# Expert network of a transformer block: tokens sorted by expert, weights picked by register, rows moved by indirect DMA

## The chip, the cores and the metric

The kernel runs on one core of one Trainium2 chip. The metric is the device time of one execution in microseconds. Engines: PE (TensorE), DVE (VectorE), ACT (ScalarE), POOL (GpSimd) and SP (SyncE); SP and POOL also issue DMAs. SBUF is the on-chip memory, PSUM holds PE's results.

## What is computed

A block of a transformer in fp32 over x of 8 x 512 tokens with 128 channels: layer norm, causal attention of 16 heads of 8 with relative key and value tables, projection, residual; then layer norm and an expert network of 8 experts, of which each token uses 2, beside 2 shared experts that every token uses.

```python
x = x + attn(layernorm(x))
xt = layernorm(x).reshape(-1, 128)                      # 4096 tokens
scores = softmax(xt @ gate_w.T)
_, idx = top_k(scores + gate_bias, 2)
weights = take_along_axis(scores, idx, axis=1)
for e in range(8):
    gate_e = sum(where(idx == e, weights, 0.0), axis=1)
    y = y + gate_e[:, None] * ((silu(xt @ w1[e].T) * (xt @ w3[e].T)) @ w2[e].T)
z = silu(xt @ sw1.T) * (xt @ sw3.T) @ sw2.T             # 2 x 128 hidden channels
x = x + y + z
```

## The kernel before

Attention works on pairs of batches (GB = 2, so G = 4 groups) and on rows of 128 queries (NI = 4), which makes 16 pairs e of a group and a row. A pair has 8 quads q of four heads; a quad is cut into units m by the width of its row (one unit in row 0, two in row 1, four in rows 2 and 3), 352 units in all. Every engine's program is one loop over slots m, written out at build time. In slot m PE turns the probabilities of unit m-3 (`tp`, L849), does what the plan `OPS[m]` holds and multiplies the scores of unit m+1 (`qk`, L837). `OPS` comes from `schedule()` (L108), which gives each operation a due slot, a rank and one of three spare PSUM banks; where a bank is taken the operation moves to a later slot. Its kinds are relative scores (`rel`), probabilities times values (`av`, L866), values of the near band (`rv`, L882), the turn of y (`yt`, `yb`) and the projection (`pj`, L905). DVE finds the minimum of the scores (L1075) and copies turned probabilities (L1060), ACT takes the exponentials (L998), copies the rest (L987) and the relative scores (L974). POOL has one job a quad, `near_probs` (L783), whose copy of the band (L795, L799) frees one of two buffers of turned probabilities: both copying engines wait for `pc_done` two quads later. SP issues every DMA in order.

Behind attention, `expert_part` (L1142) runs densely: eight chunks of 512 tokens, and in each chunk ten steps, one for each of the 2 shared and 8 routed hidden blocks. A step is two matmuls of 512 columns (`hidden`, L1357 and L1358), Silu on ACT (L1392), the product with the gate half on DVE (L1412), and the second layer as four tiles of 128 tokens (`product`, L1367; the shared blocks accumulate in one product of eight). DVE adds each expert's product, scaled by the token's gate, onto the chunk (L1427); a gate is zero where the token did not pick the expert. h1, h3 and y each have two PSUM banks. The next chunk is normalised on ACT (L1267), turned (L1275), scored (L1290), and its top two experts are found on DVE in some twenty small instructions (L1317 to L1347), all beside the steps of the chunk before. The last attention pair is finished inside the first seven steps (`last_row`). fp32 matmuls stand in the trace as two instructions each, fp32 transposes as one.

## Time and profile before

| | |
|---|---|
| runs | 776.20, 782.39, 783.75 us |
| median | 782.39 us |
| span of the profiled execution | 770.0 us |
| median less span | 12.4 us |
| PE, DVE, ACT, POOL busy in the span | 90%, 77%, 67%, 33% |

A line of the profile names a source line, an engine, what was written and read, the shape and the count, then busy time and the mean of one. Idle time before a group is put to the instruction that ended it. PE's ends are modelled, since matmuls are pipelined: the distance from start to start is what a matmul costs, and the chain of waits shows it.

### The profile page before, as it was taken

The page shows a single profiled execution, that of the slowest core. Times are in us where ns is not written, and L with a number is a line of the kernel's source. Part 1 is how long each engine was busy: PE and PEld are TensorE (multiplying, and loading weights), DVE is VectorE, ACT ScalarE, POOL GpSimd, SP SyncE. Part 2 cuts the span into 40 slices and gives each one's busy share as a digit, 9 for nine tenths or more (in the row PEclk, how much of TensorE's full clock was granted, in tenths as well). Part 3 has the DMA queues.
Part 4 walks back from the last instruction along what each step waited for, and adds up shares of the span by engine and source line. Part 5 has one row for each costly group of instructions (what it writes and reads, how often), then busy time and mean ns, then how long its engine had stood idle before and what let it go on. Part 6 is the DMA issues. An engine that isn't in the chain of part 4 may idle for free. (4 is left out here: it accounts for less than half of the span.)

```text
span 770.0 us, 27094 instructions
## 1 busy us (share of the span) xinstructions
PE 690.5 (90%) x10316; PEld 507.9 (66%) x10368; DVE 589.2 (77%) x2036; ACT 514.7 (67%) x1032; POOL 255.8 (33%) x253
## 2 busy tenths in 40 slices
...
POOL 9443445334355534545543445533000000000000
...
GB/s 255 262 295 335 333 303 264 203 244 277 309 250 302 255 222 253 249 238 241 236 222 266 221 232 255 271 153 50 3 22 28 29 5 23 28 15 1 14 15 14
DMA packets 117839, 138.48 MB, mean 180 GB/s; under 512 B 8976, under 2 KB 86288, under 8 KB 117520
## 3 DMA queue, kind: packets, MB, share of 16 engines
...
## 5 line engine op out<-in xcount | busy, mean ns | idle before, releaser
L1075 DVE CUSTOM_DVE_ANT_0 ps<-ps,near 128x128 f32<-128x128 f32 (+3 forms) x512 | 245.1, 509 | 90.5 <-PE ps L837 57.0
L998 ACT ACTIVATE work<-ps,nmin 128x128 f32<-128x128 f32 (+3 forms) x512 | 248.4, 548 | 54.2 <-DVE nmin L1075 49.4
L849 PE MATMUL ps<-ident,work 128*128 128x128 f32 x1280 | 202.6, 278 | 20.7 <-issue 11.6
L849 PEld LDWEIGHTS ps<-ident,work 128*128 128x128 f32 x1280 | 157.0, 143 | 36.5 <-issue 13.7
L795 POOL TENSOR_SCALAR_AFFINE_SELECT work<-work 128x512 f32<-128x512 f32 x96 | 61.5, 641 | 237.8 <-ACT work L987 203.6
L1392 ACT ACTIVATE near<-ps 128x512 f32<-128x512 f32 x80 | 47.5, 595 | 133.3 <-PE ps L1357 133.2
L799 POOL TENSOR_TENSOR work<-work 128x512 f32<-128x512 f32 x96 | 124.2, 1294 | 8.0
L1060 DVE COPY work<-ps 128x512 f32<-128x512 f32 (+1 forms) x192 | 123.2, 642 | 2.5 <-issue 1.6
L837 PE MATMUL ps<-kb,qb 128*128 128x384 bf16 (+3 forms) x460 | 110.6, 298 | 12.3 <-ACT work L998 9.4
L1367 PEld LDWEIGHTS ps<-work,near 128*128 128x128 f32 x640 | 82.6, 192 | 34.2 <-issue 31.6
L987 ACT ACTIVATE work<-ps 128x512 f32<-128x512 f32 (+1 forms) x160 | 90.2, 564 | 18.7 <-PE ps L849 18.1
L866 PE MATMUL ps<-work,vb 128*9 128x128 f32 x2560 | 96.1, 277 | 4.2 <-ACT relS L974 2.6
L1412 DVE TENSOR_TENSOR near<-near,ps 128x512 f32<-128x512 f32 x80 | 54.9, 687 | 50.3 <-ACT near L1392 36.4
L974 ACT ACTIVATE relS<-ps 128x512 f32<-128x512 f32 x128 | 84.4, 660 | 11.6 <-PE ps L824 10.2
L1367 PE MATMUL ps<-work,near 128*128 128x128 f32 x640 | 83.2, 275 | 0.0
L1357 PE MATMUL ps<-near,work 128*128 128x512 f32 x160 | 82.8, 599 | 0.0
L1358 PE MATMUL ps<-near,work 128*128 128x512 f32 x160 | 81.8, 593 | 0.0
L1427 DVE SCALAR_TENSOR_TENSOR near<-ps,near 128x128 f32<-128x128 f32 x256 | 71.9, 343 | 5.3
L866 PEld LDWEIGHTS ps<-work,vb 128*9 128x9 f32 x2560 | 57.7, 91 | 26.5 <-issue 19.7
L1075 DVE DVE_READ_ACCUMULATOR2_ANT nmin<- 128x1 f32 x512 | 72.1, 141 | 0.0
L882 PE MATMUL ps<-tv,work 128*32 128x8 f32 x4096 | 59.3, 179 | 12.1 <-issue 11.9
L882 PEld LDWEIGHTS ps<-tv,work 128*32 128x32 f32 x4096 | 48.2, 112 | 30.5 <-issue 27.3
...
## 6 DMA issues: line engine op xcount, KB each, us to landing
...
w_slots<-relS SPq DMA_DIRECT2D x128, 256.0 KB, 4.5
qk_rows<-work SPq DMA_DIRECT2D x36, 256.0 KB, 4.7
near<-w_slots SPq DMA_DIRECT2D x32, 256.0 KB, 4.6
qk_rows<-y SPq DMA_DIRECT2D x9, 256.0 KB, 6.8
...
```

Source lines behind the costliest of these rows:

```text
L799: nc.gpsimd.tensor_tensor(dst, ptmp[:, :, :], pT[:, q % 2, :, i * P:(i + 1) * P], ALU.add).then_inc(pc_done, 1)
L837: ins = nc.tensor.matmul(qk_ps[:, m % 3, h * wide:(h + 1) * wide], qb[:, n, i * P:(i + 1) * P], kb[:, n // 4 * 2 + n % 2, 0:wide], start=T ...
L849: ins = nc.tensor.transpose(tp_ps[:, m % 2, n * P:(n + 1) * P], prob[:, m % PROBS, n * P:(n + 1) * P], ident[:, :])
L866: ins = nc.tensor.matmul(bank[32 * h:32 * h + VD, a * P:(a + 1) * P], vb[:, g % 2, b * NI + j, n * VD:(n + 1) * VD], pT[:, q % 2, h, j * P ...
L882: ins = nc.tensor.matmul(bank[32 * tq:32 * tq + NH, a * D:(a + 1) * D], pcT[:, e % 2, tau, :], tv[:, tau, :], start=True, stop=True)
L974: nc.scalar.activation(relS[:, q % RSLOTS, :, :, :].rearrange("p a j h -> p a h j"), misc("rel", q).rearrange("p (a h j) -> p a h j", a=2, ...
L987: nc.scalar.activation(pT[:, q % 2, n * w:n * (w + 1), 0:wide], tp_ps[:, m % 2, 0:n * wide].rearrange("p (h s) -> p h s", h=n), ACT.Copy). ...
L998: ins = nc.scalar.activation(prob[:, m % PROBS, h * wide:(h + 1) * wide], qk_ps[:, m % 3, h * wide:(h + 1) * wide], ACT.Exp, bias=nmin[:, ...
L1060: nc.vector.tensor_copy(pT[:, q % 2, n * w:n * (w + 1), 0:wide], tp_ps[:, m % 2, 0:n * wide].rearrange("p (h s) -> p h s", h=n)).then_inc( ...
L1075: nc.vector.tensor_tensor_reduce(out=scores, in0=scores, in1=near[:, q % NEAR, a, 4 * P - wide:4 * P, r], scale=1.0, scalar=3e38, op0=ALU. ...
L1357: nc.tensor.matmul(h1_ps[k % 2], w1_sb[:, m, :], rhs, start=True, stop=True).then_inc(h1_ready, 1)
L1367: ins = nc.tensor.matmul(y_ps[k % 2][:, n * P:(n + 1) * P], hT[:, (NM * c + m) % 4, n * P:(n + 1) * P], w2_sb[:, m, :], start=(m == ms[0]) ...
```

## The change

The eight routed experts no longer run over all tokens.

- The tokens are taken in three segments: groups 0 and 1 (16 tiles of 128), group 2 (8) and group 3 (8). Within a segment every token's two rows are placed by expert; an expert's rows start at a multiple of 128, so that each tile of 128 rows has one expert. The number of tiles is that of the worst padding: 39, 23 and 23, in units of four tiles 10, 6 and 6, 22 units in all.
- Normalising moves into attention and to POOL (`normalise`: a root by `pow` and a Newton step in small links, then two instructions of 128x128 a pair), for each pair e. SP stores the normalised rows (`xn_dram`), PE turns them (`xt`) and scores them (`gl`) as new entries of the plan, ACT copies the turned rows (stored to `xnT_dram`) and DVE the scores.
- `route` on DVE, once a segment in 19 steps, finds the two experts, the gates, and each row's place: a running sum over tiles, two matmuls for the sum over the 128 partitions (`rk`), and the experts' starts. For segments 0 and 1 it is spread over slots 217 to 238 and 305 to 326 of attention; for segment 2 it is in the tail. Thirty entries of the old plan move by one to three slots.
- POOL scatters the rows: each indirect DMA takes one tile of 128 rows of 512 bytes, for one of the two picks. 32 and 16 of them stand behind the quads 88 to 101 and 120 to 125, up to three a quad, and the last 16 behind attention.
- The tail first runs the 22 sorted units: load, turn (4 transposes), weights of each tile copied by ACT from an offset read into a register (`pick_weights`, four reads and four copies of 128x384), 8 hidden matmuls of 128 columns, Silu, multiply, 4 products, copy, store. Then 16 shared units (dense, 512 columns). POOL gathers the products back, 64 indirect DMAs, chunk by chunk, and DVE adds them with their gates (`combine`) and the shared product (`add_shared`). h1, h3 and the routed y have one PSUM bank each.
- The last attention pair runs in half-steps inside the first sorted units. Square roots on ACT, `normalise` and the exponentials on ACT in the tail but one go away. All expert weights come in one DMA late in attention.

```diff
+SEGMENTS = [(0, 2), (2, 3), (3, 4)]
+SEG = len(SEGMENTS)
+SEG_TILES = [GB * NI * (hi - lo) for lo, hi in SEGMENTS]
+SEG_AT = [GB * NI * lo for lo, hi in SEGMENTS]
+SORTED = [-(-((TOPK * n * P + E * (P - 1)) // P) // 4) for n in SEG_TILES]
+SORTED_AT = [sum(SORTED[:s]) for s in range(SEG + 1)]
+NSORT = SORTED_AT[SEG]
+MOST = max(SEG_TILES)
+SEG_ROWS = GB * 2 * len(Q_PART) * D * H * T * 2 // (4 * C)
...
+    for e in range(LATE):
+        due.append((NORM_AT[e] + 6, 4, ("xt", e)))
+        due.append((NORM_AT[e] + 8, 4, ("gl", e)))
+    for s in range(SEG - 1):
+        due.append((route_slot(s) + 12, 4, ("rk", s)))
...
+SPREAD = [3, 3, 3, 3, 2, 2, 0, 0]
+
+
+def scatters():
+
+    at, q = [[] for q in range(NQ)], 0
+    for s in range(SEG - 1):
+        while q % QUADS or row(q) < 2 or last(q) + 4 < SLOT_OF["rk", s] + 5:
+            q += 1
+        for n in range(TOPK * SEG_TILES[s]):
+            while len(at[q]) >= SPREAD[q % QUADS] or row(q) < 2:
+                q += 1
+            at[q].append((s, n))
+        q += 1
+    return at
+
+
+SCATTER = scatters()
...
+                    for s, n in SCATTER[q]:
+                        experts["scatter"](pool, s, n)
+                experts["normalise"](pool, GI - 1, x1[:, (GI - 1) % 2, :, :], x1_done)
+                for n in range(TOPK * SEG_TILES[SEG - 1]):
+                    experts["scatter"](pool, SEG - 1, n)
+                experts["pool"](pool)
 
...
+                def last_row(half):
 
                     e = GI - 1
-                    if step < 2:
-                        if step == 0:
-                            for kind, *what in LAST:
-                                pe.wait_ge(*READ[kind](*what))
-                            experts["scores"](pe, 0)
-                        for c in range(RVN // 2 * step, RVN // 2 * (step + 1)):
+                    if half < 2:
+                        for c in range(RVN // 2 * half, RVN // 2 * (half + 1)):
                             rv(e, c)
-                    if step in (2, 3):
-                        if step == 2:
-                            experts["wait_turned"](pe, 0)
-                            pe.wait_ge(rvn_done, GI)
-                        else:
-                            experts["wait_scores"](pe, 0)
-                        yt(e, step - 2)
-                    if step == 4:
+                        (xt, gl)[half](LATE)
+                    if half == 2:
+                        yt(e, 0)
+                        yt(e, 1)
+                    if half == 4:
                         yb(e)
-                    if step == 5:
+                    if half == 6:
                         pj(e)
-                    if step == 6:
-                        pe.wait_ge(ynT_done, GI)
-                        pe.wait_ge(x1_done, GI)
+                    if half == 9:
+                        xt(e)
+                    if half == 10:
+                        gl(e)
+                    if half == 16:
+                        rk(SEG - 1)
 
...
+                def last_row(half):
+
+                    s = SEG - 1
+                    if half == 1:
                         near_values(GI - 1)
-                    if step in (2, 3):
-                        normalise(GI - 1, step - 2)
-                    if step == 6:
+                    if half == 3:
+                        experts["copy_scores"](dve, LATE, misc("gl", LATE))
+                        normalise(GI - 1, 0)
+                        normalise(GI - 1, 1)
+                    if half == 7:
                         residual(GI - 1)
-
-                experts["vector"](dve, last_row)
-
-
-def expert_part(nc, ctx, t, ps, x1_dram, gate_w, gate_bias, w1, w3, w2, out):
-    NM = NSH + E
-    CT = CH // P
-    CHUNKS = TILES // CT
-    NY = E + 1
-    AC = 1 + CT * E
+                    if half == 11:
+                        experts["copy_scores"](dve, GI - 1, misc("gl", GI - 1))
+                    if 12 <= half < 16:
+                        for step in ((0,), (1, 2, 3), (4, 5, 6), (7, 8, 9))[half - 12]:
+                            experts["route"](dve, s, step)
+                    if half == 16:
+                        experts["route"](dve, s, 10)
+                    if half in (17, 18):
+                        for step in ((11, 12, 13, 14), (15, 16, 17, 18))[half - 17]:
+                            experts["route"](dve, s, step, misc("rk", s))
+
...
+    def normalise(pool, e, x1, x1_done):
+        if e == 0:
+            pool.wait_ge(const_in, 16)
+            nc.gpsimd.memset(pa[:, 0:pad, :], 0.0)
+            nc.gpsimd.memset(pb[:, 0:pad, :], 0.0)
+        links = [6 * e]
+
+        def then(ins):
+            links[0] += 1
+            ins.then_inc(root, 1)
+            pool.wait_ge(root, links[0])
+
+        pair = tile_pair(e)
+        pool.wait_ge(mv_done, GB * (e + 1))
+        then(nc.gpsimd.tensor_scalar(stat[:, 0, :], mv[:, pair, 1], EPS, None, ALU.add))
+        then(nc.gpsimd.tensor_tensor(stat[:, 1, :], stat[:, 0, :], mhalf, ALU.pow))
+        then(nc.gpsimd.tensor_tensor(stat[:, 2, :], stat[:, 1, :], stat[:, 1, :], ALU.mult))
+        then(nc.gpsimd.tensor_tensor(stat[:, 2, :], stat[:, 2, :], stat[:, 0, :], ALU.mult))
+        then(nc.gpsimd.tensor_scalar(stat[:, 2, :], stat[:, 2, :], -0.5, 1.5, ALU.mult, ALU.add))
+        nc.gpsimd.tensor_scalar(stat[:, 3, :], mv[:, pair, 0], -1.0, None, ALU.mult)
+        then(nc.gpsimd.tensor_tensor(stat[:, 1, :], stat[:, 1, :], stat[:, 2, :], ALU.mult))
+        if x1 is None:
+            pool.wait_ge(xp_in, 16 * EARLY)
+            x1 = xnp[:, e % XN, :, :]
+        else:
+            pool.wait_ge(x1_done, e + 1)
+        if e >= XN:
+            pool.wait_ge(xn_out[e % XN], 16 * (e // XN))
+            pool.wait_ge(xt_ready, e - XN + 1)
+        for b in range(GB):
+            ins = nc.gpsimd.tensor_scalar(xnp[:, e % XN, b, :], x1[:, b, :], stat[:, 3, b:b + 1], stat[:, 1, b:b + 1],
+                                          ALU.add, ALU.mult)
...
+    def scatter(pool, s, n):
+        k, r = SEG_AT[s] + n // TOPK, n % TOPK
+        c = k // NI
+        if n == 0:
+            pool.wait_ge(pos_done, s + 1)
+        if n % (TOPK * NI) == 0:
+            pool.wait_ge(ring_in[c % 2], 16 * (c // 2 + 1))
+        nc.gpsimd.indirect_dma_start(out=sorted_rows, out_offset=bass.IndirectOffsetOnAxis(ap=pos[:, r, k:k + 1], axis=0),
+                                     in_=ring[:, c % 2, k % NI, :], in_offset=None).then_inc(sc_out[c % 2], 16)
 
     def pool_program(pool):
-        for e in range(E):
-            ins = nc.gpsimd.memset(order[:, e:e + 1], float(E - e))
-        ins.then_inc(order_done, 1)
+        for j in range(SORTED_AT[SEG - 1], SORTED_AT[SEG - 1] + XS):
+            load_sorted(pool, j)
+        for s in range(SEG):
+            for n in range(2):
+                pool.wait_ge(y_out[n], 16 * len(range(n, SORTED_AT[s + 1], 2)))
+            for k in range(SEG_AT[s], SEG_AT[s] + SEG_TILES[s]):
+                for r in range(TOPK):
+                    nc.gpsimd.indirect_dma_start(out=yg[:, TOPK * k + r, :], out_offset=None, in_=y_rows[s],
+                                                 in_offset=bass.IndirectOffsetOnAxis(ap=loc[:, r, k:k + 1], axis=0)
+                                                 ).then_inc(yg_in[k // NI], 16)
 
...
+    def tensor_program(pe, last_row):
+        def turn(j):
+            wait_sorted(pe, j)
+            wait(pe, xTs_done, j)
+            for n in range(4):
+                ins = nc.tensor.transpose(tT_ps[:, n * P:(n + 1) * P], xs[:, j % XS, n, :], t["ident"][:, :])
+            ins.then_inc(tT_ready, 1)
+
+        def hidden(j):
+            pe.wait_ge(xTs_done, j + 1)
+            pe.wait_ge(wq_done, j + 1)
+            for w, bank in ((0, h1_ps), (1, h3_ps)):
+                wait(pe, (silu_done, hT_done)[w], j)
+                for n in range(4):
+                    ins = nc.tensor.matmul(bank[:, n * P:(n + 1) * P], wq[j % WQ][:, n, w, :],
+                                           xT[:, j % 2, n * P:(n + 1) * P], start=True, stop=True)
+                ins.then_inc((h1_ready, h3_ready)[w], 1)
+
+        def product(j):
+            pe.wait_ge(hT_done, j + 1)
+            wait(pe, ys_done, j)
+            for n in range(4):
+                ins = nc.tensor.matmul(y_ps[:, n * P:(n + 1) * P], hT[:, j % 2, n * P:(n + 1) * P], wq[j % WQ][:, n, 2, :],
+                                       start=True, stop=True)
+            ins.then_inc(y_ready, 1)
+
+        def hidden_all(u):
+            c, m = divmod(u, NSH)
+            if m == 0:
+                pe.wait_ge(xa_in[c // GB], 32 * GB)
+            for w, bank in ((0, h1_ps), (1, h3_ps)):
+                pe.wait_ge((silu_done, hT_done)[w], NSORT + u)
+                nc.tensor.matmul(bank, ws[:, w, m, :], xnT_all[:, c, :], start=True, stop=True
+                                 ).then_inc((h1_ready, h3_ready)[w], 1)
+
+        def product_all(c):
+            pe.wait_ge(hT_done, NSORT + NSH * (c + 1))
+            if c < 2:
+                pe.wait_ge(ys_done, NSORT)
+            else:
+                pe.wait_ge(acc_done, AC * (c - 1))
+            for n in range(4):
+                for m in range(NSH):
+                    ins = nc.tensor.matmul(ps[:, 4 + c % 2, n * P:(n + 1) * P], hT[:, (NSH * c + m) % 4, n * P:(n + 1) * P],
+                                           ws[:, 2, m, :], start=(m == 0), stop=(m == NSH - 1))
+            ins.then_inc(z_ready, 1)
+
+        turn(0)
+        for j in range(NSORT):
+            if j + 1 < NSORT:
+                turn(j + 1)
+            last_row(2 * j)
+            hidden(j)
+            last_row(2 * j + 1)
+            if j:
+                product(j - 1)
+        for u in range(UNITS2):
+            hidden_all(u)
+            if u == 0:
+                product(NSORT - 1)
+            elif u % NSH == 0:
+                product_all(u // NSH - 1)
+        product_all(B - 1)
+
...
+    def pick_weights(act, j):
+        s = SEG_OF[j]
...
+            act.wait_ge(w_in, 16)
+            offsets.extend(act.alloc_register(f"offset{n}") for n in range(4))
+        if j == SORTED_AT[s]:
+            act.wait_ge(ids_done, s + 1)
+        act.load(offsets, ids[0:1, 4 * j:4 * j + 4])
+        wait(act, y_ready, j - WQ + 1)
+        for n in range(4):
+            at = act.snap(offsets[n], min_val=0, max_val=3 * P * (E - 1))
+            ins = nc.scalar.activation(wq[j % WQ][:, n, :, :].rearrange("p w c -> p (w c)"), wx[:, bass.ds(at, 3 * P)], ACT.Copy)
+        ins.then_inc(wq_done, 1)
 
     def scalar_program(act, last_row):
-        exponentials(act, 0)
-        for k in range(NM * CHUNKS):
-            act.wait_ge(h1_ready, k + 1)
-            wait(act, hT_done, k - 1)
-            nc.scalar.activation(silu[:, k % 2, :], h1_ps[k % 2], ACT.Silu).then_inc(silu_done, 1)
-            last_row(k)
-            if k == NM * (CHUNKS - 4):
-                roots(act, 1)
-            for j in due(k, "normalise"):
-                normalise(act, j)
-            for j in due(k, "copy"):
-                copy_turned(act, j)
-            for j in due(k, "exp"):
-                exponentials(act, j)
-
-    def vector_program(dve, last_row):
-        def hidden(c, m):
-            k = NM * c + m
-            dve.wait_ge(silu_done, k + 1)
-            dve.wait_ge(h3_ready, k + 1)
-            if k >= 4:
-
-                cb, mb = divmod(k - 4, NM)
-                dve.wait_ge(y_ready, NY * cb + max(mb - 1, 0) + 1)
-            nc.vector.tensor_tensor(hT[:, k % 4, :], silu[:, k % 2, :], h3_ps[k % 2], ALU.mult).then_inc(hT_done, 1)
-
-        def add(c, u):
-            k = NY * c + u
-            dve.wait_ge(y_ready, k + 1)
+        def gate(j):
+            act.wait_ge(h1_ready, j + 1)
+            wait(act, hT_done, j - 1)
+            nc.scalar.activation(sl[:, j % 2, :], h1_ps, ACT.Silu).then_inc(silu_done, 1)
+
+        for j in range(NSORT):
+            if j + 1 < NSORT:
+                pick_weights(act, j + 1)
+            gate(j)
+            last_row(j)
...
+        def combine(c, half):
+            if half == 0:
+                dve.wait_ge(yg_in[c], 16 * TOPK * NI)
+                dve.wait_ge(xa_in[c // GB], 32 * GB)
+            for r in range(TOPK):
+                for n in range(2):
+                    k = NI * c + 2 * half + n
+                    if r:
+                        dve.wait_ge(acc_done, AC * c + 4 * half + n + 1)
+                    nc.vector.scalar_tensor_tensor(out=x1_all[:, k, :], in0=yg[:, TOPK * k + r, :], scalar=gates[:, r, k:k + 1],
+                                                   in1=x1_all[:, k, :], op0=ALU.mult, op1=ALU.add).then_inc(acc_done, 1)
+
```

## Rows read from the trace of the kernel before

**Rows 1.** The page, part 2: POOL's busy tenths in 40 slices of 19.25 us.
```profile
POOL 9443445334355534545543445533000000000000
```
**Rows 2.** Windows by stage: stretch, length, busy us (instructions) of each engine, PEclk, DMA share, GB/s.
```profile
20.00:40.00 20.00, 13.87 (x60) 8.63 (x60) 18.82 (x67) 13.11 (x20) 8.53 (x4) 0.87 0.90 266
...
400.00:500.00 100.00, 92.50 (x1935) 72.79 (x1936) 85.78 (x315) 87.14 (x194) 49.15 (x51) 1.00 0.84 249
...
634.00:662.00 28.00, 28.00 (x135) 18.07 (x133) 19.80 (x65) 13.19 (x21) 0.00 (x0) 1.00 0.07 20
```
**Rows 3.** Chain of waits, 634.9 to 665 us: start, us, the piece of the chain.
```profile
635.13 1.78 PE ps L1367 x16
636.91 0.44 PE ps L1275 x4
637.35 0.86 PE ps L1357 x2
...
639.07 0.89 PE ps L1367 x8
...
642.57 0.79 PE ps L1290 x8
...
662.56 1.84 PE ps L1367 x16
```
**Rows 4.** Timeline, PE, the first dense expert matmul: start, us, instruction, shape, count.
```profile
540.10 1.13 PE L1357 MATMUL ps<-near,work 128*128 128x512 f32 x2
```
**Rows 5.** Timeline, the end of the span.
```profile
764.16 0.69 DVE L1412 TENSOR_TENSOR near<-near,ps 128x512 f32<-128x512 f32 x1 [0.65 <-ACT near L1392]
764.99 2.23 DVE L1427 SCALAR_TENSOR_TENSOR near<-ps,near 128x128 f32<-128x128 f32 x8
767.25 0.37 SPq L1233 DMA_DIRECT2D out<-near  x1
```
**Rows 6.** Waits, 130 to 500 us: total us, times, longest.
```profile
DVE ps L1075 <- PE ps L837: 43.4, 62, 2.2
ACT work L998 <- DVE nmin L1075: 34.6, 52, 1.6
```
**Rows 7.** ACT: timeline at 605 us, then groups by shape (busy us, mean ns).
```profile
605.65 1.64 ACT L1267 ACTIVATE near<-vb,work,rstd 128x128 f32<-128x128 f32 x4
...
L987 ACT ACTIVATE work<-ps 128x512 f32<-128x512 f32 x87 | 52.1, 598 | 12.1 <-PE ps L849 11.4
L1015 ACT ACTIVATE work<-ps 128x256 f32<-128x256 f32 x15 | 5.8, 390 | 1.8 <-PE ps L898 1.8
...
L1392 ACT ACTIVATE near<-ps 128x512 f32<-128x512 f32 x80 | 47.5, 595 | 133.3 <-PE ps L1357 133.2
L1392 ACT ACT_TABLE_LOAD x9 | 11.5, 1283 | 0.2
```
**Rows 8.** Timeline, ACT's last copy of attention.
```profile
540.23 0.60 ACT L1010 ACTIVATE y<-ps 128x512 f32<-128x512 f32 x1 [0.42 <-PE ps L866]
```
**Rows 9.** DMA issues: KB each, median us from issue to landing.
```profile
out<-near SPq DMA_DIRECT2D x8, 256.0 KB, 2.3
...
vb<-x_dram SPq DMA_DIRECT2D x6, 256.0 KB, 3.1
```
**Rows 10.** DVE, small instructions: a group by shape, then one line's min/median/max ns.
```profile
L1325 DVE TENSOR_TENSOR near<-near 128x32 f32<-128x32 f32 x8 | 1.5, 192 | 0.3
...
L1100 DVE TENSOR_TENSOR work<-work,rden x32: 291/293/1404, 125.1 to 556.1; 128x128 f32<-128x128 f32 x32
```
**Rows 11.** POOL: timeline of its quads, a group, one line's min/median/max.
```profile
384.99 0.64 POOL L795 TENSOR_SCALAR_AFFINE_SELECT work<-work 128x512 f32<-128x512 f32 x1 [2.97 <-ACT work L987]
...
417.47 0.63 POOL L795 TENSOR_SCALAR_AFFINE_SELECT work<-work 128x512 f32<-128x512 f32 x1 [3.86 <-DVE work L1060]
...
L355 POOL TENSOR_TENSOR work<-work 128x1024 bf16<-128x1024 f32 x6 | 12.8, 2159 | 11.5 <-ACT work L448 11.5
...
L799 POOL TENSOR_TENSOR work<-work x96: 1277/1293/1388, 58.2 to 539.7; 128x512 f32<-128x512 f32 x96
```

728 lines of the change are left out of this document (445 added, 283 removed).

## Prediction

> **What bounds the kernel now.** I read the page's slices first, then the windows by stage, then the chain of waits, and last the waits of the middle. In the slices GpSimd (POOL) is busy until about slice 27 of 40 and then stands at zero: the kernel has two stages, attention up to about 540 us and the expert network behind it [rows 1]. The windows say how the two differ. At 400 to 500 us PE, DVE and ACT are all busy 86 to 93% and the DMA engines 84%; at 634 to 662 us PE is busy all of the time, ACT under half, POOL not at all, the DMA engines 7% [rows 2]. The chain of waits then shows what a dense expert step costs. One chunk of 512 tokens goes from one x16 product (635.13) to the next (662.56): 27.43 us, with ten hidden steps (0.86 for w1, the same for w3), one shared product of 1.78, eight expert products of 0.89, one turn of 0.44 and one score of 0.79: 17.2 + 1.78 + 7.12 + 0.44 + 0.79 = 27.3. Nothing but PE is on it [rows 3]. Eight chunks are 219 us. The first such matmul starts at 540.10 [rows 4]; the last additions start at 764.99, the last store is issued at 767.25, and the trace ends at 770.0 [rows 5]. So the tail is 229.9 us and PE-bound, and fewer products are worth their whole PE time there.
>
> In attention no engine has room of its own: DVE waits for PE 43 us, ACT for DVE 35 us in the 370 us from 130 to 500 [rows 6]. It is a balanced loop, in which work added to any of the three shows in part.
>
> **The sum.** I write the new time as 540.1 (attention now) + a loss in attention + the new tail, and add 12.4 us, by which the median of the runs (782.39) lies above the span (770.0).
>
> **What goes.** 80 hidden steps, 64 expert products and the gate work leave the tail. Sorting needs 22 units of four tiles of one expert each (10 + 6 + 6; the count is fixed by the worst padding), and 16 shared units (two per chunk) stay dense.
>
> **PE of the new tail.** A sorted unit has 4 transposes, 8 hidden matmuls of 128 columns and 4 products. The x8 product entry is four fp32 tiles in 0.89, so the unit is 0.44 + 3 x 0.89 = 3.11 us. Small tiles cost little here: four of 128 columns take 0.89 where one of 512 takes 0.86 [rows 3]. The shared part of a chunk is 4 x 0.86 + 1.78 = 5.22.
>
> **ACT of the new tail.** Each sorted unit copies the weights of four tiles, 128x384 each, in SBUF. Four SBUF-to-SBUF instructions of 128 columns take 1.64 and so stand about 0.4 apart; from 256 to 512 columns a PSUM copy grows by 0.21, so 384 columns add 0.21 and a copy takes 0.60 of the queue. Four are 2.4, Silu 0.5 to 0.6 [rows 7]: 3.0 us, beside PE's 3.11. Unpriced is the reading of four registers from SBUF ahead of them, which no row shows. Its bounds are 0 (ACT's queue still holds copies to run) and, by the nearest fetch that stops ACT, the table load of 1.28 [rows 7]. The banks for h1 and h3 are also single now, so PE waits for Silu. I take 3.7 us a unit, between 3.1 and 4.4. That is 22 x 3.7 = 81.
>
> **Compute path.** The first unit waits for its weight copies behind ACT's last copy at 540.23 (0.6, then 2.4, then about 1 for registers): 4 us [rows 8]. Add 81; 3 for last-row work on PE (rv, yt, pj, the last turns and scores) that the looser loop does not hide; the shared part at 8 x 5.6 = 45 (5.22 and a wait for Silu per chunk); and 4 behind the last matmul (0.69 for the add, 0.37 for the issue, 2.3 for the store's landing [rows 5, 9]). 4 + 81 + 3 + 45 + 4 = 137 us against 229.9. DVE fits: three instructions of 0.69 in a sorted unit, and in a shared chunk eight additions (eight take 2.23 now), two multiplies and one add, 4.3 of 5.6 [rows 5].
>
> **Indirect DMAs on POOL, the price that decides.** The tail holds 16 scatters and 64 gathers, all on one in-order queue, none in the trace of before. Call the queue time of one c. The last segment's positions come with half-step 18 of the sorted loop, that is 9.5 units in: 4 + 9.5 x 3.7 + 3 = 42 us. Then 16c; 4 us for landing and the four sorted loads (a 256 KB load lands in 3.1 [rows 9]); 64c; 2.5 for the last landing (store 2.3 [rows 9]); 7.5 for the last chunk's eight additions, the shared add and the store. Queue path: 56 + 80c. The nearest rows for c are 0.37 (SP issuing a store), 0.63 and 1.29 (one POOL instruction over 128x512) and 2.16 (the longest repeated POOL instruction, 128x1024) [rows 5, 11]. An indirect DMA must be worked out row by row for 128 rows by POOL itself, so the POOL rows are nearer than SP's; I take 1.2 between 1.29 and the shorter ones, and keep 0.4 and 2.16 for the range. At 1.2 the queue path is 152 us, longer than the compute path by 15; they cross at c = 1.01. So the tail is set by POOL's gathers: combine(c) waits for eight gathers a chunk, 9.6 us, where PE needs 5.6. The Trainium skill ("DMA: Bandwidth & Descriptors", Specifications) gives about 1 us to the first byte of a DMA issued from GpSimd; with c = 1.0 the queue path would be 136 and the compute path would end last. No run here shows it yet.
>
> PE then idles over a third of the shared stage. The trace has windows in which PE was busy 69% and the granted clock was 0.87, against 1.00 where it was busy all the time [rows 2]; where the clock falls to 1.2 GHz a chunk's 5.22 becomes up to 10.4, hardly over 9.6. I count it as up to 6 us in the range, not in the sum.
>
> **Attention.** PE gets 14 row pairs of two transposes (0.22) and two score matmuls (a quarter of 0.79 and a load: up to 0.44): 9 us. DVE gets 14 copies and twice about 39 small routing instructions: 0.19 for 128x32 and 0.29 for two SBUF inputs of 128x128 [rows 10], with some 0.03 between them and wider ones for both picks at once, so 13 us for the segment of 16 tiles, 10 for that of 8, 26 with the copies. ACT gets 14 copies of 0.39 [rows 7] and loses two square roots: 3 us. If all of it fits into waits the loss is 0, if PE's and DVE's add up it is 35. DVE has 14 us idle in 100 [rows 2], but the routing comes in bursts of 19 slots that its slack doesn't cover. The DMA engines go from 84% busy to about 90% with some 9 MB more (scatters, stored and reloaded rows). I take 15.
>
> POOL in attention: a quad's own work is 2.0 us (0.63 + 1.29) and quads of the long rows come 5.4 us apart (six in 384.99 to 417.47) [rows 11]. Scatters go up to three behind a quad, 16 a row of eight quads (43 us): 16 + 16c + 6 for two normalisations of about 3. At c = 1.2 that is 41, just inside; it breaks at c = 1.3, and behind a late POOL wait both the copies of the probabilities (pc_done) and PE's turn of the normalised rows. So POOL's work there costs nothing at 1.2, and three rows' overrun, 3 x (16c - 21), above 1.3.
>
> **Sum:** 540.1 + 15 + 152 + 12.4 = 719.5. I predict 720 us, 8% faster.
>
> **Rivals.**
> 1. POOL's DMAs are cheap (c at most 1.0): the compute path ends last. 540.1 + 15 + 137 + 12.4 = 705, and 683 with nothing lost in attention and 3.3 us a unit. For it: a queue that only writes descriptors need not touch 128x512 elements. Against: the POOL rows.
> 2. The register reads stop ACT: 5 us a unit, 110 for the 22, compute path 166, queue path 54 + 96 + 14 = 164. 733. For it: four reads and four addresses a unit stand on ACT's queue in front of copies that PE needs. Against: they can be done while copies run.
> 3. Attention pays 40 rather than 15, since PE waits in line for POOL's rows: 745.
> 4. The slower side: the POOL queue is dear. Its place is the 48 scatters in attention and the 80 DMAs of the tail; the time is 567.5 + 56 + 80c + 48c - 63, equal to 782 at c = 1.73. If each issue also had to wait for one DVE instruction of 0.69, c = 1.2 + 0.69 = 1.9 and the time 804. For it: DVE and POOL do disturb each other, a 128x128 product of two SBUF operands (as in the routing and in combine) takes 0.29 in the median and up to 1.40 [rows 10]. Against: POOL's own 128x512 work keeps to 1.28 to 1.39 there, beside a busy DVE [rows 11]. The Trainium skill ("SBUF — State Buffer", Who interferes with whom) speaks for it: DVE instructions that take both ports keep GpSimd from writing descriptors until they end. Most of DVE's operands here come from PSUM, to which that rule doesn't apply.
> That the change doesn't do what it says has no case: the counts of units are fixed numbers.
>
> **Chances.** Forecast (c from 1.05 to 1.5, 708 to 752) 0.45; rival 1 0.22; rival 2 0.09; rival 3 0.10; rival 4 0.14. The range leaves out rival 4's slower part and the best of rival 1: 685 to 780. Runs of one kernel spread by 1%, so about 1% is what can be told from no change. Rivals 1 to 3 and the forecast are faster by more than that; rival 4 gives 0.12 slower and 0.02 within: 0.85, 0.03, 0.12. Forecast's own range: 708 to 752.
>
> **What would show it.** Each indirect DMA 1.2 us apart on POOL, POOL the releaser of combine in the last 60 us and PE idle there; sorted units 3.7 us apart with ACT busy over 80%; attention ending near 555. Wrong would be: additions that never wait for gathers (rival 1), units 5 us apart (2), pc_done or xn_done among the long waits (3), scatters 1.7 us or more apart (4).

## The result: slower by 7.6%

The kernel after takes 838.85 us (median of 4 runs, 835.08 to 841.95) against 781.4 us for the kernel before beside it (776.2 to 783.75). The ratio on record, of the fast runs of both kernels, is 1.076, with a 95% interval from 1.068 to 1.084 (the two medians alone divide to 1.074). The prediction was 720 us and "faster". The profiled execution has a span of 833.3 us; before it was 770.0 us.

First the page of the kernel after: the span, the slices (20.8 us each) and the groups of the two new operations. The answer to [rows 1] is the POOL line: GpSimd now works until 800 us.

```profile
span 833.3 us, 27048 instructions
PE   4686789999789999887789867878878647144967
DVE  7875668886778787888868467977745623021546
ACT  3686767887778788875557467756665514031211
POOL 8453444344668444654568666445831065745430
PEclk9998999999989999999899999989999888566989
L1507 POOL DMA_INDIRECT sorted_rows<-work x64 | 62.7, 980 | 44.5 <-DVE work L1642 28.1
L1518 POOL DMA_INDIRECT near<-y_rows,work x64 | 60.8, 950 | 43.2 <-DMA y_rows<-work 24.3
```

Two things stand out. The indirect DMAs are as cheap on GpSimd as forecast: 0.95 to 0.98 us each and 0.30 between two. And in slices 35 to 37 (about 708 to 771 us) PE, DVE and ACT all fall to 0 to 4 tenths while GpSimd is at 4 to 7: next to nobody else works. The granted clock falls with them, to 0.5 and 0.6.

The timeline of PE gives the borders of the stages (answering [rows 4]): the first turn of a sorted unit, and the first and last products of the dense shared stage.

```profile
610.70 0.63 PE L1659 MATMUL ps<-ident,kb 128*128 128x128 f32 x4 [0.92 <-ACT y L1129]
773.42 1.88 PE L1686 MATMUL ps<-qb 128*128 128x512 f32 x4
825.12 1.88 PE L1686 MATMUL ps<-qb 128*128 128x512 f32 x4
```

So attention ends at 610.7 us, not at 540.1, and the tail takes 222.6 us, of 229.9 before: 163 for the 22 sorted units and 60 for the shared part. The forecast had 555 and 152.

The windows of these two stages and of the 32 gathers of the first segment (stretch, length, busy us of PE, PE weight load, DVE, ACT, POOL, then PEclk, DMA share, GB/s; compare the dense stage in [rows 2]), then the waits of the last of these stretches:

```profile
696.00:736.00 40.00, 11.40 (x82) 10.22 (x81) 4.43 (x7) 5.51 (x12) 30.32 (x32) 0.65 0.45 123
610.00:773.00 163.00, 93.46 (x891) 88.30 (x892) 53.50 (x116) 55.88 (x118) 69.49 (x80) 0.76 0.43 121
773.00:833.00 60.00, 47.50 (x206) 27.04 (x204) 34.95 (x91) 9.55 (x16) 15.37 (x16) 0.94 0.23 62
```

```profile
DVE work L1762 <- remote: 25.3, 1, 25.3
ACT y L1738 <- remote: 11.5, 1, 11.5
POOL near L1518 <- issue: 9.8, 32, 0.3
```

In those 40 us PE is busy 11.4, DVE 4.4 and ACT 5.5. "remote" stands for a release that the trace cannot find: one multiplication of DVE waited 25.3 us although every instruction it needs had been recorded as ended long before (PE's matmuls at 703.8 us, ACT's Silu at 718.6; the multiplication starts at 735.6). That is the loss, and the experiments are about what it is.

### The profile page after: what moved, and what is told of

Its sections match the earlier page's. It is cut to its first block and busy times, and to the rows that moved or that the text cites. A ratio compares the mean times of both kernels' runs of the same rounds, so it can differ in the third digit from the quotient of the medians.

```text
span 833.3 us, 27048 instructions
## 1 busy us (share of the span) xinstructions
PE 644.8 (77%) x10228; PEld 494.5 (59%) x10228; DVE 545.8 (65%) x1821; ACT 495.7 (59%) x1031; POOL 426.5 (51%) x523
## 5 line engine op out<-in xcount | busy, mean ns | idle before, releaser
L963 PE MATMUL ps<-ident,work 128*128 128x128 f32 x1280 | 210.4, 285 | 29.7 <-ACT work L1106 18.6
L963 PEld LDWEIGHTS ps<-ident,work 128*128 128x128 f32 x1280 | 160.7, 146 | 57.6 <-ACT work L1106 25.3
L951 PE MATMUL ps<-kb,qb 128*128 128x128 bf16 (+3 forms) x512 | 132.6, 311 | 16.7 <-ACT work L1117 13.9
L1185 DVE COPY work<-ps 128x512 f32<-128x512 f32 (+1 forms) x192 | 123.4, 642 | 27.0 <-POOL work L907 19.2
L1093 ACT ACTIVATE relS<-ps 128x512 f32<-128x512 f32 x128 | 84.5, 661 | 15.5 <-PE ps L938 11.9
L1507 POOL DMA_INDIRECT sorted_rows<-work x64 | 62.7, 980 | 44.5 <-DVE work L1642 28.1
L1518 POOL DMA_INDIRECT near<-y_rows,work x64 | 60.8, 950 | 43.2 <-DMA y_rows<-work 24.3
L980 PEld LDWEIGHTS ps<-work,vb 128*9 128x9 f32 x2560 | 58.9, 92 | 30.2 <-issue 22.2
L996 PE MATMUL ps<-tv,work 128*32 128x8 f32 x4096 | 63.8, 181 | 16.3 <-issue 15.0
L1762 DVE TENSOR_TENSOR work<-y,ps 128x512 f32<-128x512 f32 x38 | 26.1, 687 | 75.9 <-remote 31.8
L1738 ACT ACTIVATE y<-ps 128x512 f32<-128x512 f32 x38 | 22.5, 593 | 84.1 <-remote 40.8
L951 PEld LDWEIGHTS ps<-kb,qb 128*128 128x128 bf16 x512 | 42.5, 101 | 37.1 <-ACT work L1117 20.2
L938 PE MATMUL ps<-te,qb 128*128 128x128 bf16 x512 | 51.9, 226 | 10.6 <-ACT relS L1093 7.0
L938 PEld LDWEIGHTS ps<-te,qb 128*128 128x128 bf16 x512 | 35.5, 100 | 26.5 <-issue 14.8
```

Source lines behind the costliest of these rows:

```text
L938: ins = nc.tensor.matmul(bank[:, h * P:(h + 1) * P], qb[:, 4 * u + h, i * P:(i + 1) * P], te[:, :], start=True, stop=True)
L951: ins = nc.tensor.matmul(qk_ps[:, m % 3, h * wide:(h + 1) * wide], qb[:, n, i * P:(i + 1) * P], kb[:, n // 4 * 2 + n % 2, 0:wide], start=T ...
L963: ins = nc.tensor.transpose(tp_ps[:, m % 2, n * P:(n + 1) * P], prob[:, m % PROBS, n * P:(n + 1) * P], ident[:, :])
L980: ins = nc.tensor.matmul(bank[32 * h:32 * h + VD, a * P:(a + 1) * P], vb[:, g % 2, b * NI + j, n * VD:(n + 1) * VD], pT[:, q % 2, h, j * P ...
L996: ins = nc.tensor.matmul(bank[32 * tq:32 * tq + NH, a * D:(a + 1) * D], pcT[:, e % 2, tau, :], tv[:, tau, :], start=True, stop=True)
L1093: nc.scalar.activation(relS[:, q % RSLOTS, :, :, :].rearrange("p a j h -> p a h j"), misc("rel", q).rearrange("p (a h j) -> p a h j", a=2, ...
```

## Experiments

Each time below is that of one run, beside one run of the kernel before on the same chip (777.2 us for the first four, 777.1 or 776.7 for the others). The kernel after was timed beside 781.4, so differences of a few microseconds from its 838.9 say nothing.

### Are the gathers to blame, or do they only make room? Gathers last

GpSimd waits for all sorted products before the first gather.

```
-        for s in range(SEG):
-            for n in range(2):
-                pool.wait_ge(y_out[n], 16 * len(range(n, SORTED_AT[s + 1], 2)))
+        for n in range(2):
+            pool.wait_ge(y_out[n], 16 * len(range(n, NSORT, 2)))
+        for s in range(SEG):
```

> The changed kernel with one difference: POOL starts its 64 gathers only when all 22 sorted products are stored, not segment by segment. Theory A (while DMAs whose descriptors POOL writes are in flight, DVE and ACT start instructions late although all they wait for is done): the units after the 16 scatters take about 3.5 us instead of the 9 us they took beside gathers, the sorted units end near 710 us instead of 780, and the 80 us of gathers then stand behind them: about 815 us in all. Theory B (the sorted units are slow by themselves: single PSUM banks, register reads, stores of products): the sorted units still end near 780, the gathers come on top, and the time is near 875.

854.8 us, against 777.2 for before on the same chip. The windows, with the border of the two stages at 719 us:

```profile
610.00:719.00 109.00, 85.46 (x893) 82.85 (x894) 53.58 (x116) 55.52 (x118) 24.04 (x32) 0.87 0.52 152
719.00:852.00 133.00, 54.73 (x203) 31.40 (x202) 34.92 (x91) 9.55 (x16) 60.78 (x64) 0.69 0.19 52
```

The sorted stage fell from 163 to 109 us once the gathers had left it, and the shared stage, which got all 64 of them, rose from 60 to 133. The loss goes where the gathers go. The total lies between the two expectations (815 and 875), so it did not decide by itself; the stages did: the sorted units end at 719, near theory A's 710 and far from theory B's 780.

### The same gathers in the kernel before

Here nothing of the change is made. 64 indirect gathers of 64 KB are added to GpSimd, which has nothing to do there, from the third dense chunk on. They go from the input into a buffer of attention that is free by then, and nobody reads them. The cut leaves out the load of the indices.

```
+    def extra(pool):
+        pool.wait_ge(spots_in, 16)
+        pool.wait_ge(acc_done, AC * 2)
+        for k in range(64):
+            nc.gpsimd.indirect_dma_start(out=spare[:, k, :], out_offset=None, in_=x_rows,
+                                         in_offset=bass.IndirectOffsetOnAxis(ap=spots_sb[:, k:k + 1], axis=0)
+                                         ).then_inc(extra_done, 16)
```

> The kernel before, with 64 indirect gathers of 128 rows of 512 bytes (from the input x into an SBUF buffer that nothing reads) added on POOL, which is idle there, from the third dense chunk on. The dense steps themselves are unchanged. Theory A: PE, DVE and ACT wait with nothing to wait for while the gathers run (80 us), and the time grows by 30 us or more, to 810 or above. Theory B: the dense steps keep their 27.4 us a chunk and the time stays within 3 us of before, 782.

Two controls move the same bytes at the same place with plain descriptors. In the first GpSimd issues them; in the second SP does.

```
-            nc.gpsimd.indirect_dma_start(...)
+            pool.dma_start(spare[:, k, :], x_rows[P * (k % 32):P * (k % 32 + 1), :]).then_inc(extra_done, 16)
```

> As the run with 64 added gathers, but each DMA is a plain one from POOL (64 KB of consecutive rows of x, no index). Theory A in the form that any DMA with descriptors written by POOL does it: the same loss as with gathers, 30 us or more. In the form that the index reading or the scattered rows do it: no loss, within 3 us of before. Theory B: no loss.

> As the run with 64 added plain DMAs, but issued by SP at the same place, same rows and size (0.4 us each, about 26 us in all). Theory A: no loss, since POOL writes nothing: within 3 us of before. Rival C (many DMAs of 512-byte rows, whoever issues them, hold up code or semaphores): a loss of 10 us or more.

| added to before | us | against before (777.2) |
|---|---|---|
| 64 indirect gathers, GpSimd | 850.6 | +73 |
| 64 plain DMAs, GpSimd | 776.3 | 0 |
| 64 plain DMAs, SP | 775.9 | 0 |

73 us for 64 gathers is 1.14 us each, where each takes 1.25 us of GpSimd's queue: the other engines lose nearly all the time for which gathers run. Neither the bytes nor GpSimd as the issuer explain it; what is left is the indirect form. (The plain ones came faster, 0.53 us apart, so a slower pace was no relief to them.) The windows of the kernel with indirect gathers: ahead of them and among them; then the same place with plain DMAs by GpSimd.

```profile
580.00:600.00 20.00, 20.00 (x100) 13.21 (x99) 14.20 (x48) 11.23 (x19) 0.00 (x0) 1.00 0.10 27
...
640.00:660.00 20.00, 3.10 (x9) 1.51 (x7) 0.96 (x4) 0.00 (x0) 15.12 (x17) 0.59 0.20 53
```

```profile
620.00:640.00 20.00, 20.00 (x89) 12.34 (x90) 15.33 (x55) 8.98 (x15) 20.00 (x39) 1.00 0.49 128
```

PE goes from full to 3.1 of 20 us, with the DMA engines at 20%. Beside plain DMAs it stays full with them at 49%.

The timeline of the held kernel tells more. The trace shows an fp32 matmul as two instructions; I call each a pass. First three rows of PE, then who waited for each, on DVE and ACT:

```profile
638.84 2.08 PE L1385 MATMUL ps<-work,near 128*128 128x128 f32 x8 [14.18 <-DVE near L1430]
640.71 1.53 PE L1375 MATMUL ps<-near,work 128*128 128x512 f32 x2
642.08 1.02 PE L1376 MATMUL ps<-near,work 128*128 128x512 f32 x2
```

```profile
659.04 1.12 DVE L1445 SCALAR_TENSOR_TENSOR near<-ps,near 128x128 f32<-128x128 f32 x4 [20.26 <-remote]
665.35 0.60 ACT L1410 ACTIVATE near<-ps 128x512 f32<-128x512 f32 x1 [30.97 <-remote]
671.00 0.69 DVE L1430 TENSOR_TENSOR near<-near,ps 128x512 f32<-128x512 f32 x1 [10.51 <-remote]
```

DVE reads the result of the eight passes 18 us after they are recorded as ended, ACT that of the next two 23 us after, DVE that of the last two 28 us after. Two more passes cost about 5 us, eight about 20: some 2.5 us a pass. PE itself had started 0.06 us after DVE's multiplication of 638.09 ended at 638.78. This suggested that it is the matmuls that are held, and that DVE and ACT only wait for them. It could also be that PE's signal alone comes late; the next experiment tells the two apart.

### Which engine is held? A kernel of twenty phases

> A kernel of its own that computes nothing of the reference (its output is a copy of x). Twenty short phases, one after the other, each a fixed pattern of work alone and then the same pattern while GpSimd issues 20 DMAs of 64 KB (about 25 us at the 1.25 us apart of the two kernels): chained 128x512 copies on VectorE from SBUF and from PSUM, the same on ScalarE, a ping-pong between VectorE and ScalarE, a stream of 64 f32 matmuls that nobody reads between, ten rounds of four matmuls with a VectorE copy (or a ScalarE copy) of the result behind them, the same with bf16 matmuls; and the f32 rounds once more beside plain DMAs, indirect scatters, gathers of rows in order and gathers of 64 rows. In e2_dense_gathers three rows in a chain (8, 2 and 2 matmuls) were seen by the engine that waits 18.1, 23.1 and 27.9 us after their start, 2.3 us for each matmul. Theory M (a matmul is held, the other engines are not): the patterns without TensorE keep their pace to 10%, each with TensorE shows about 2.3 us for one matmul while the gathers run, so three of the ten rounds in 25 us where alone a round takes under 2.5 us. Theory S (a wait on another engine's semaphore is held): the ping-pong slows as much as the rounds with TensorE, the chains on one engine don't. Theory E (every engine's start is held): the chains on VectorE and ScalarE slow to over 2 us a step. In all, the plain DMAs cost nothing, and scatters cost what gathers cost; if it goes by rows, half the rows cost half.

The chains on VectorE kept their pace: 48 copies of 128x512, half of them beside gathers, 0.48 us apart from SBUF (beside nine gathers) and 0.73 from PSUM (beside 13). ScalarE's 24 copies took 15.83 us alone and 15.83 beside gathers.

The stream of 64 f32 matmuls (128 passes) that nobody reads shows the hold in PE's own rows. The first row is the stream alone; the others are from the stream beside gathers, which run from 204.5 to 229.2 us:

```profile
186.39 17.21 PE L66 MATMUL ps<-a,w 128*128 128x128 f32 x128 [169.68 <-DMA near<-in_x,at]
203.86 9.67 PE L66 MATMUL ps<-a,w 128*128 128x128 f32 x84 [0.26 <-PE ps L66]
...
230.03 0.37 PE L66 MATMUL ps<-a,w 128*128 128x128 f32 x1 [1.03 <-issue]
231.43 0.37 PE L66 MATMUL ps<-a,w 128*128 128x128 f32 x1 [1.03 <-issue]
232.14 5.21 PE L66 MATMUL ps<-a,w 128*128 128x128 f32 x24 [0.34 <-issue]
```

The first 84 passes are 0.12 us apart. From the eighth gather on, at 213.8 us, the next 20 take 18.4 us, 0.92 each, and from 232.1 on the last 24 are 0.22 apart, at a granted clock of 0.73. No engine reads in between and PE waits for none, so it is the passes themselves that are held and not the signal behind them.

The rounds with a reader did not keep their pace either. ScalarE's rows of one phase, whose gathers run from 305.80 to 330.5 us:

```profile
310.99 0.28 ACT L59 ACTIVATE c<-ps 128x128 f32<-128x128 f32 x1 [1.31 <-issue]
312.94 0.28 ACT L59 ACTIVATE c<-ps 128x128 f32<-128x128 f32 x1 [1.68 <-PE ps L66]
316.55 0.28 ACT L59 ACTIVATE c<-ps 128x128 f32<-128x128 f32 x1 [3.33 <-remote]
324.40 0.28 ACT L59 ACTIVATE c<-ps 128x128 f32<-128x128 f32 x1 [7.57 <-issue]
334.29 0.28 ACT L59 ACTIVATE c<-ps 128x128 f32<-128x128 f32 x1 [9.61 <-remote]
336.80 0.28 ACT L59 ACTIVATE c<-ps 128x128 f32<-128x128 f32 x1 [2.23 <-PE ps L66]
```

A round holds four f32 matmuls, which the trace shows as eight passes. It takes 1.59 us up to the fifth gather, then 1.95, 3.6, 7.9 and 9.9 us; once the gathers are over it is at 2.5 us, which is also what a round takes alone at the lower granted clock (285.87 to 288.38 us, clock 0.56). At 9.9 us for eight passes a pass costs 1.2 us, about half of the 2.3 expected. Scatters (rounds of 3.6, 6.4 and 9.9 us from 402.2 on) and gathers of rows in order (3.8, 6.4 and 9.9 from 436.1 on) do the same, so neither the direction nor the addresses matter. Gathers of 64 rows take GpSimd hardly less (0.90 against 0.95 us) and held PE too (2.6 and 7.1 us in two rounds, before GpSimd stood still for 3.4 us); whether half the rows hold it less is open. Theory M holds, with half its price. The bf16 rounds had ended 9 us into their gathers, too soon to tell.

### What kind of matmul, and what resets it

> A kernel of its own that computes nothing of the reference (its output is a copy of x), in the manner of p1_probe with longer phases and 24 DMAs of 64 KB beside each. In p1_probe the chains of VectorE and ScalarE and their ping-pong kept their pace, only the f32 matmuls were held: from the eighth or ninth gather on, a round of 8 passes whose result VectorE waits for took 7.5 to 9.6 us instead of 1.25, about one pass for each gather; after GpSimd had stood still for 3.4 us the rounds were at 1.5 to 2.5 us again. The bf16 rounds were over before the eighth gather. Expected here. Theory B (backlog: it takes about eight gathers without a pause to hold TensorE, and a pause resets it): bf16 rounds and transposes slow down as the f32 matmuls do from the eighth gather on; with GpSimd waiting for the landing after each, every second, every fourth or every sixth gather, the 20 rounds stay at 1.5 to 2.5 us each; with a 128x512 copy between the gathers, or a plain DMA for every second gather, they are held less or not at all; the ping-pong of VectorE and ScalarE stays at 1.1 us for the whole 30 us. Theory F (it is the f32 pass): the bf16 rounds stay at 1.0 us throughout. Theory T (time, not backlog: it begins 10 us after the first gather and stays): pauses for the landing change nothing.

Distance of the rounds on VectorE while 24 DMAs go out, read from its timeline:

| pattern and GpSimd's pace | alone | beside the gathers |
|---|---|---|
| f32 matmuls, gathers 1.25 us apart | 1.54 | 1.5, then 1.95, 2.9, 4.3, 9.1, 9.1 from the sixth gather on |
| bf16 matmuls, the same | 0.99 | 1.0, then 3.1, 2.2, 3.5, 4.9, 7.0, 4.2 |
| f32 transposes, the same | 1.50 | 1.5, then 1.7, 2.8, 4.9, 7.0, 4.9 |
| VectorE and ScalarE in turn, no PE | 1.12 | 1.25 to the end |
| f32, a wait for the landing after each (2.77 us a gather) | 1.54 | 1.54 |
| f32, after every second (2.0) | 1.54 | 1.54 |
| f32, after every fourth (1.63) | 1.54 | 1.54 |
| f32, after every sixth (1.5) | 1.54 | 1.54, two rounds of 2.1 and 2.6 |
| f32, a 128x512 copy of GpSimd between two (1.88) | 1.54 | 1.54 |
| f32, a plain DMA between two (1.86; 12 of each, and GpSimd stood still for 3.5 us after the sixth pair) | 1.54 | 1.54 |

VectorE's rows of the first phase (gathers from 50.2 to 80.0 us) and of the bf16 phase (138.7 to 168.5 us):

```profile
65.84 0.29 DVE L54 COPY b<-ps 128x128 f32<-128x128 f32 x1 [3.97 <-remote]
74.95 0.29 DVE L54 COPY b<-ps 128x128 f32<-128x128 f32 x1 [8.82 <-remote]
84.06 0.29 DVE L54 COPY b<-ps 128x128 f32<-128x128 f32 x1 [8.82 <-remote]
86.52 0.29 DVE L54 COPY b<-ps 128x128 f32<-128x128 f32 x1 [2.17 <-PE ps L65]
```

```profile
161.28 0.29 DVE L54 COPY b<-ps 128x128 f32<-128x128 f32 x1 [4.62 <-remote]
168.28 0.29 DVE L54 COPY b<-ps 128x128 f32<-128x128 f32 x1 [6.71 <-remote]
172.48 0.29 DVE L54 COPY b<-ps 128x128 f32<-128x128 f32 x1 [3.90 <-remote]
173.47 0.29 DVE L54 COPY b<-ps 128x128 f32<-128x128 f32 x1 [0.70 <-PE ps L65]
```

9.11 us for eight passes is 1.14 us a pass. A round of bf16 matmuls or transposes has four passes, and at 7.0 us they cost 1.75 each, so the price is not one and the same for every pass. Theory B is right: every kind of matmul is held, from the fifth gather of an unbroken row on at the earliest (f32 in the first probe) and from the eleventh at the latest (transposes), and not where the gathers come 1.6 us apart or more on average. Whether it is the pause or the average pace that counts, these phases do not separate; the row with plain DMAs in between proves least, since it had only 12 gathers. Theory F (only f32) and theory T (pauses don't help) fall. What in the chip carries this backlog, no run here shows.

### In the kernel itself: without the early scatters, and with plain DMAs throughout

The kernel after without the 48 scatters in attention:

```
-                    for s, n in SCATTER[q]:
-                        experts["scatter"](pool, s, n)
...
```

The waits for these scatters go too.

> The kernel after without the 48 scatters of the first two segments, which go out in the attention stage (the rows of these segments are then not there, so the output is wrong; all else stays). After stands at 838.9, its attention stage ends at 610 us instead of 540 of before. Theory A (an indirect DMA holds the other engines back for about its 1.1 us): 48 x 1.1 = up to 53 us back at most, at least half of it, the attention ends at 560 to 585 and the kernel takes 790 to 812. Theory N (the attention pays for the normalisation on GpSimd in its order, and for the routing): the attention still ends beyond 595, 825 to 838 us.

814.6 us: 24 us back for 48 scatters, 0.5 us each. That is just outside both expectations (790 to 812, and 825 to 838), but attention ends at 584.3, inside theory A's 560 to 585. That an early scatter costs less than a gather of the tail fits with their order, up to three between other work of GpSimd; no run tests it by itself.

Then each of the 128 indirect DMAs becomes a plain one of the same 64 KB, with the rows in order.

> The kernel after with each of its 128 indirect DMAs replaced by a plain DMA of the same 64 KB issued by GpSimd at the same place, rows in order (so the output is wrong; waits and buffers stay). Theory A: the 64 gathers give back 1.14 us each as in e2_dense_gathers (73), the 16 late scatters 15, the 48 early ones 25 to 50: 838.9 - 113 to 138 = 700 to 726 us, sorted units 3.1 to 4 us apart. Rival R (registers, picks and the chain of three products set the pace of the sorted units): the tail stays over 200 us behind the attention's end, 780 us or more.

743.3 us, with before at 777.1: with the same bytes, waits and order, but plain descriptors, the kernel is 4% faster than before. This edit takes away two things at once: what an indirect DMA does to PE, and what it costs GpSimd's own queue (0.53 us apart instead of 1.25). Its attention ends at 588.3 and its tail takes 152.4 us of the span of 740.7. It stayed 17 us above the range expected: the tail gave back 70 us where I had allowed 88, and attention 22 where I had allowed 25 to 50. Its windows, attention from 130 us on, sorted stage, shared stage:

```profile
130.00:588.00 458.00, 394.53 (x7883) 309.73 (x7935) 363.23 (x1266) 341.65 (x719) 252.34 (x373) 0.96 0.78 232
588.00:691.00 103.00, 82.84 (x889) 80.44 (x890) 53.07 (x116) 55.30 (x118) 39.18 (x75) 0.92 0.62 184
691.00:740.00 49.00, 45.41 (x207) 26.68 (x206) 35.36 (x91) 9.55 (x16) 11.45 (x22) 1.00 0.32 91
```

Between two sorted units that wait for nothing there are 3.11 us (the turns at 625.24, 628.35 and 631.47), which is just PE's own work. The other intervals are 3.3 to 11 us, the longest of them beside attention's last row.

### The other loss in attention: GpSimd's order

That attention ends at 588.3 instead of 540.1 even with plain DMAs has to do with something else. The waits of that kernel, 130 to 588 us:

```profile
DVE work L1185 <- POOL work L907: 19.9, 8, 5.0
...
ACT work L1106 <- POOL work L907: 15.5, 7, 5.8
...
POOL work L1480 <- DVE mv L1527: 45.8, 10, 7.8
```

None of these waits is in the trace of before. The new normalisation stands ahead of the near part of the same quad on GpSimd, and it waits for VectorE's moments: 45.8 us in ten waits. The near part behind it is then late, and DVE stops for it 8 times, 19.9 us in all. The experiment puts it behind:

```
+                    near_probs(q)
                     for e in range(GI - 1):
                         if q == NORM_BEFORE[e]:
                             experts["normalise"](pool, e, ...)
-                    near_probs(q)
```

> The kernel after with GpSimd's normalisation of a pair of tiles moved behind the near part of the same quad instead of ahead of it, nothing else. In after, GpSimd stands 60 us in nine such waits for VectorE's moments, 3.5 to 6.5 us each, and ScalarE and VectorE then wait 5 us each for the near part. Theory N: most of these waits no longer delay anything, the attention ends 15 to 35 us earlier, 805 to 825 us. Theory A (the indirect DMAs are all of it): within 5 us of after, 834 to 844.

840.9 us, no gain: as theory A had it, but not for its reason. The waits for the near part did go (DVE's from 19.2 in after to 4.0 us), and another took their place; DVE's waits, 130 to 610 us:

```profile
DVE ps L1200 <- remote: 43.4, 25, 3.7
DVE ps L1200 <- PE ps L951: 43.1, 55, 2.4
...
DVE work L1185 <- POOL work L907: 4.0, 2, 2.2
```

The "remote" waits were 15.8 us in after. I read it so: without its pauses GpSimd sends the scatters in tighter rows and PE is held more. That is argued and not shown, since some waits are "remote" without any indirect DMA too (11.9 us in before, 13.9 in the kernel with plain DMAs, the longest 2.4). The expectation's 60 us in nine waits also counted one of 21.2 us behind attention; in attention after had 39.0 us in eight. The next one leaves the indirect DMAs out, with both edits:

> The kernel after with plain DMAs instead of the indirect ones (as in e6_plain_dmas, the output is wrong) and with GpSimd's normalisation behind the near part of the quad (as in e7_normalise_after). In e6_plain_dmas the attention ends at 588.3: 48 us behind before, of which VectorE's own added work is 27 and its waits for a late near part 20. In e7_normalise_after these waits went, but the waits for held matmuls grew by 28. Theory N: with nothing held the waits for the near part are won, the attention ends at 566 to 574 and the time is 720 to 731. Rival: the loop is balanced, other waits take their place, 583 to 590 and 738 to 745.

729.1 us, attention ends at 573.7, both inside the range expected: 14.6 us from the order alone, now that nothing is held.

### Pauses in the kernel

GpSimd waits for the landing after every fourth indirect DMA.

```
+        if n % 4 == 0 and n:
+            pool.wait_ge(sc_out[...], <the count with the scatter before>)
+                    if (g + 1) % 4 == 0 and g >= 0:
+                        pool.wait_ge(yg_in[g // (TOPK * NI)], 16 * (g % (TOPK * NI) + 1))
```

> The kernel after, with GpSimd waiting after every fourth indirect DMA until it has landed, nothing else. After is at 838.9, with plain DMAs instead of indirect ones it is at 743.3. Each wait adds about 1.5 to 2.5 us to GpSimd's queue: four in the last scatters, sixteen in the gathers, so the queue path of the tail grows from 152 by up to 50. Theory B (a pause resets the backlog): the other engines run at their pace, the sorted stage takes 85 to 110 us instead of 163, the time is 760 to 790. Theory T (pauses don't help): 850 to 890.

> Both changes of order together, with the indirect DMAs kept: GpSimd waits after every fourth of them, and normalises behind the near part. All of the reference is computed. Theory B with N: 10 to 20 us less than e8_paced4, 745 to 775, faster than the kernel before. If the waits for the landing make the near part late again in the attention stage: no less than e8_paced4. Theory T: over 850.

826.2 and 819.1 us, with before at 776.7. Both beat the kernel after, neither the kernel before; both missed the range expected. Theory B is right about PE: the sorted stage takes 117 us instead of 163 (85 to 110 expected). But now GpSimd's queue ends last, as its chain of waits says (page of the first of the two):

```profile
POOL 6%; DMA 5%; issue 3%; PE 0%; DVE 0%; POOLq 0%
POOL near L1524 6%; DMA near<-y_rows,work 5%; PE ps L1703 0%; POOL sorted_rows L1510 0%; POOL kb L1435 0%; POOLq L731 0%; DVE work L1784 0%; DVE work L1791 0%; DVE work L1768 0%; POOLq L1523 0%
```

Four gathers take 6.6 us with their wait, so the 64 take 106 us instead of 80. In the second kernel they start at 700.7, when the 16 late scatters are out, and the last goes out at 806 us of a span of 817.4. No version here that computes the whole reference beats before. An estimate from these rows: six gathers between pauses would give some 8 us (1.5 instead of 1.63 for each of 64), and GpSimd's idle time between 635.7 and 664.1 us, if gathers could fill all of it, 28 more. From 817.4 that is a span of 781, still more than the 776.7 us that before takes as a whole.

## Why the prediction was wrong, step by step

The forecast span was 540.1 + 15 + 152 = 707.1; measured was 833.3, so 126.2 us are to be found. They close:

| step | forecast | measured | difference |
|---|---|---|---|
| attention, own work and waits without order and held PE | +15 | +33.6 (573.7 - 540.1) | 18.6 |
| attention, GpSimd's order | 0 | 14.6 (588.3 - 573.7) | 14.6 |
| attention, indirect instead of plain | 0 | 22.4 (610.7 - 588.3) | 22.4 |
| tail with plain DMAs | 152 | 152.4 | 0.4 |
| tail, indirect instead of plain | 0 | 70.2 (222.6 - 152.4) | 70.2 |

The rows are differences of single runs, taken in this order of removal; in another order they would differ (the order of GpSimd's work is worth 14.6 us with plain DMAs, and 2.2 us of attention with indirect ones, 610.7 to 608.5). "Indirect instead of plain" holds both the held PE and the dearer queue.

**What bounds before** was right, and so was the work saved: with plain DMAs the tail falls from 229.9 to 152.4 us.

**Price of an indirect DMA on GpSimd's queue:** 1.2 us taken, 1.25 measured (0.95 and 0.30). Rival 4, the slower side, put the flip at 1.73 us, so it was right in sign by another mechanism than its own. The Trainium skill's rule for DVE and GpSimd's descriptors ("SBUF — State Buffer", Who interferes with whom) has no price here: in attention, beside a busy DVE, the scatters took 0.96 us in the median and 1.29 at most. The trace agrees with it only faintly, in the first probe: beside DVE's chain of copies from SBUF to SBUF five of nine gathers took 1.04 to 1.10 us, and once the chain was over each took 0.94 or 0.95.

**The step that failed** is the unspoken one in "compute path" and "queue path": that the two run beside each other and the longer one counts. I asked what GpSimd pays for an indirect DMA and never what the others pay while it runs. While unbroken rows of them run, a pass of PE costs 0.9 to 2.5 us, so the paths nearly add instead of overlapping: 64 gathers beside a stage that PE bounds cost 73 us, and in the tail the sorted stage takes 163 us instead of the 103 it takes with plain DMAs.

**Queue path,** a second step, mis-sized: 56 + 80c is 156 us at c = 1.25. Two of its terms were too small. The last segment's scatters start 58.9 us behind the end of attention where nothing is held (647.2 - 588.3), not 42, and from the last of them to the first gather it is 9.2 us, not 4. An estimate with these two, the price of 1.25 us and 10 us behind the last gather (10.3 in the first run with pauses) gives 58.9 + 20 + 9.2 + 80 + 10 = 178 us. So of the tail's 70.2 us some 44 are held matmuls (222.6 - 178) and some 26 the queue's own length. It also means that freeing PE alone would have given a span of about 588.3 + 178 = 766 us, hardly below the 775 of before.

**Compute path:** forecast at 137, of which 88 up to the end of the sorted stage. Measured without held matmuls: 103 and 49. The shared part was right (45 + 4). A sorted unit on its own is at 3.11 us, cheaper than my 3.7; 22 of them are 68 us, and the other 35 us of the 103 lie in the longer intervals. PE's waits in this stage come to 20.5 us: 4.8 for loads of sorted rows, 4.6 for one step of the routing on DVE, 3.0 for the last rows normalised by GpSimd, the others 2.3 and less. PE is busy for 82.8 us, so the rest is work, that of attention's last row, and a granted clock of 0.92. The forecast had 7 us for the start and the last row and 13 in the dearer units. The tail's 0.4 in the table is thus luck: with plain DMAs, less than half as dear on GpSimd, it is the compute path that ends it, 15 us over forecast, and it happens to meet a queue path that was forecast for another price.

**Register reads (rival 2):** no. Four weight copies take 1.76 us and a unit that waits for nothing 3.11, so the reads cost ACT nothing that shows. ACT is busy 54% there, not over 80.

**Attention:** DVE's added work, priced at 26 us, is 26.7 (363.2 against 336.5 us busy from 130 us on). Taking about half of it as hidden was too hopeful: 33.6 are lost beside the two other causes. The claim that GpSimd's work there "costs nothing at 1.2" looked at the sum of its work (41 us in 43) and not at its order; a wait of 4.6 us in the mean at the head of an in-order queue was worth 14.6 us. The prediction's own rule, to name what is queued behind a wait, was not applied to the wait for the moments. Rival 3 named this place, at the price of 25 us, and its sign, pc_done among the long waits, was there (5.0 us the longest); but it had PE waiting in line for POOL's rows, where it was DVE and ACT that waited for the near part.

**What would show it** asked for indirect DMAs 1.2 us apart and they were: a sign that was right in a kernel 119 us off. The others failed: sorted units came 7.4 us apart in the mean, not 3.7, with ACT busy 34% of the stage, attention ended at 610.7, and no addition waited for a gather in the last 60 us. The prediction gave no sign for how the other engines would fare beside indirect DMAs.
